# A two-layer graph network on one core: an early scatter into a small array, and a later one spread over five chunks

## What is computed

```python
# layer 0
h1..h4 = per-node-type linear maps of x              # 3125 x 64 each
w5e    = per-edge-type linear map of the 16 edge features
num    = sum(h3[dst] * (h4[src] + w5e), -1)
score  = softmax over an axis of length 1
out0   = h1 + segment_sum(score * (h2[src] + w5e), dst)
x      = layernorm(x + out0)
# layer 1
m      = relu(x[src] + edge_attr_32 @ We + be) + 1e-7
agg    = segment_sum(m * softmax_of_segment(m, dst), dst)
x      = layernorm(x + (x + agg) @ Wm + bm)
```

## Time and profile before

| | |
|---|---|
| runs | 2237.88, 2248.02, 2254.48 us; median 2248.02 |
| profiled execution | 2247.74 us, of it the span 2245.8 us |
| busy share of the span | TensorE 78%, VectorE 71%, GpSimd 58%, ScalarE 34% |
| mean granted TensorE clock | 0.886 |

### The profile page before, as it was taken

One profiled execution on the slowest core, in us unless ns is written; L12 is line 12 of the kernel. 1 busy time (PEld: TensorE's weight loads), 2 busy tenths in 40 slices (PEclk: granted clock), 3 DMA queues, 4 the chain that ended last, 5 costly groups with the idle time before them and its releaser, 6 DMA issues.

```text
span 2245.8 us, 29209 instructions
## 1 busy us (share of the span) xinstructions
PE 1747.1 (78%) x9112; PEld 1108.5 (49%) x9112; DVE 1602.6 (71%) x3058; ACT 757.1 (34%) x1397; POOL 1294.3 (58%) x1348
## 2 busy tenths in 40 slices
PE   6453889898889889888873487888878787878873
PEld 5222556665666556555662144454445444544442
DVE  7422677777777777677768377788778786878786
ACT  3100222222222222222222144455455545455461
POOL 6365555555666565565633666666666665656624
PEclk9876999999999999999986688899999998989885
DMA  8942444545554555454443145555545555545442
GB/s 274 369 96 83 131 137 134 156 134 154 138 150 141 144 145 144 137 146 133 139 133 93 39 117 148 148 161 153 148 147 150 150 148 143 152 144 151 144 151 57
DMA packets 220072, 323.65 MB, mean 144 GB/s; under 512 B 62802, under 2 KB 127948, under 8 KB 219789
## 3 DMA queue, kind: packets, MB, share of 16 engines
q1 hardware_dynamic: 132958, 150.94, 22.9%
q0 software_dynamic: 43056, 68.05, 13.7%
q10 hardware_dynamic: 43904, 102.79, 12.6%
HBM read 188.35 MB, written 133.22 MB: 143 GB/s over the span
## 4 chain that ended last, share of the span: by engine, by line
PE 28%; issue 17%; another core or an unknown queue 16%; ACT 12%; DVE 12%; ACTq 3%; POOL 2%; DMA 1%; DVEq 0%; SPq 0%; POOLq 0%
PE wide L957 8%; PE wide L1069 5%; ACT block L860 3%; PE wide L931 3%; PE wide L966 2%; ACTq L853 2%; ACT prob_wide L837 2%; PE wide L923 2%; ACT msg L838 2%; ACT block L841 1%; DVE h3d L1363 1%; PE bank L1005 1%; ACT block L830 1%; DVE featm L1354 1%
## 5 line engine op out<-in xcount | busy, mean ns | idle before, releaser
L672 POOL DMA_INDIRECT rows<-d_x,idx x588 | 559.7, 952 | 350.2 <-issue 155.3
L662 POOL DMA_INDIRECT block<-d_h,idx x482 | 462.9, 960 | 302.9 <-issue 126.8
L1069 PE MATMUL wide<-late,ntype_i 125*128 125x512 bf16 x975 | 240.4, 404 | 54.7 <-DVE ntype_i L1492 49.5
L662 POOL DMA_INDIRECT rows<-d_h,idx x160 | 153.8, 961 | 151.6 <-PE wide L931 58.3
L1363 DVE TENSOR_TENSOR_SCAN h3d<-keep,h3d,bank 128x512 f32<-128x512 bf16 x98 | 124.9, 1275 | 159.1 <-issue 114.4
L1069 PE MATMUL wide<-edge_lists,ntype_i 125*128 125x512 bf16 x936 | 229.2, 401 | 11.9 <-issue 11.5
L931 PE MATMUL wide<-typed,zeros 128*128 128x128 f32 (+1 forms) x1364 | 185.0, 283 | 13.1 <-issue 13.1
L1080 PE MATMUL wide<-ident,block 128*128 128x128 f32 x784 | 134.4, 320 | 72.0 <-ACT block L860 43.9
L1069 PEld LDWEIGHTS wide<-late,ntype_i 125*128 125x128 bf16 x975 | 101.1, 104 | 176.2 <-DVE ntype_i L1492 49.9
L957 PE MATMUL wide<-late,ntype_i 125*128 125x512 bf16 x702 | 177.1, 409 | 12.5 <-issue 5.0
L957 PE MATMUL wide<-edge_lists,ntype_i 125*128 125x512 bf16 (+1 forms) x702 | 170.7, 396 | 11.6 <-issue 9.2
(11 more groups left out here) (255 smaller groups left out, 3214.2 us busy)
## 6 DMA issues: line engine op xcount, KB each, us to landing
d_run<-block ACTq DMA_DIRECT2D x98, 512.0 KB
d_inj<-zeros SPq DMA_DIRECT2D x28, 896.0 KB
inj<-d_inj SPq DMA_DIRECT2D x98, 256.0 KB
d_run<-stage ACTq DMA_DIRECT2D x98, 256.0 KB
feat<-in_ea16x3T SPq DMA_DIRECT2D x196, 96.0 KB
types<-d_type SPq DMA_DIRECT2D x196, 64.0 KB
keep<-d_keep SPq DMA_DIRECT2D x196, 64.0 KB
keep<-d_pen SPq DMA_DIRECT2D x196, 64.0 KB
```

What stands on the lines that cost most here:

```text
L662: pool.indirect_dma_start(out=ring[c % RING][:, j, h, :], out_offset=None, in_=d_h24, in_offset=bass.IndirectOffsetOnAxis(ap=idx[:, c, at: ...
L672: pool.indirect_dma_start(out=rows1[c % RING1][:, j, h, :], out_offset=None, in_=d_x1, in_offset=bass.IndirectOffsetOnAxis(ap=idx[:, c, at ...
L1069: ins = pe.matmul(p_hot[s], table[q][:, SPLIT * k:SPLIT * (k + 1), :].rearrange("p b c -> p (b c)"), hot[s][:, k, :], start=(k == 0 and q ...
```

## The change

`d_early` is a second array with rows for the first 14 chunks alone (`EARLY`), cleared by 4 transfers ahead of the others (`EARLY_UNITS`). GpSimd scatters all 25 tiles into it (`early_i`; nodes whose first edge is elsewhere go to a dump row) ahead of every gather, and chunks 0 to 13 load their `inj` from it. `d_inj` loses the clearing of its first 4 transfers' rows, has 10 cleared in the head, and the last 14 in SyncE's loop, two behind each of chunks 2 to 8. The scatter into `d_inj` is 25 further DMAs, five behind the gathers of each of chunks 8 to 12. The rows of zeros are sent as 512 pieces of 448 values instead of 128 of 1792. `PICK_LEAD` falls from 4 to 2 and `FIRST_STEP` from 3 to 0. `load_pick(u)` stands ahead of the other loads of its chunk instead of behind them. ScalarE's copy of the weights into the tile of zeros waits for nothing of the clearing, and VectorE's three operations on `table` in the head stand later.

```diff
-AHEAD = 6
-ZEROS_EARLY = 7
+ZEROS_EARLY = 3
+ZEROS_LATE = 14
+EARLY = 14
+EARLY_UNITS = 4
+SCATTER_BEHIND = {c: (5 * n, 5 * n + 5) for n, c in enumerate(range(8, 13))}
...
-PICK_LEAD = 4
+PICK_LEAD = 2
...
-FIRST_STEP = 3
+FIRST_STEP = 0
...
+            no_rows = zeros[:, 0:7 * C].unsqueeze(1).to_broadcast([P, 4, 7 * C])
+
+            def clear(first, behind):
+                for z in range(first, behind):
+                    sp.dma_start(flat[z], no_rows).then_inc(s_injzero, 16)
...
-            for z in range(ZEROS_EARLY):
-                sp.dma_start(flat[z], zeros[:, :]).then_inc(s_injzero, 16)
+            for z in range(EARLY_UNITS):
+                sp.dma_start(flat_early[z], no_rows).then_inc(s_early, 16)
+            clear(EARLY_UNITS, EARLY_UNITS + ZEROS_EARLY)
...
+            def load_inj(s, r, c):
                 wait(sp, injT[s], r)
+                if c == EARLY:
+                    sp.wait_ge(s_inj, 2 * 16 * NT)
...
             for c in range(2, CHUNKS):
                 s, r = c % 2, c // 2
-                load_features0(s, r, halves(c))
-                load_inj(s, r, c * (2 * CH))
-                load_keep(s, r, halves(c))
                 for u in range(PICK_LEAD + 1, UNITS):
                     if c == max(2, UNTIL[u - LISTS] + 1):
                         load_pick(u)
+                load_features0(s, r, halves(c))
+                load_inj(s, r, c)
+                load_keep(s, r, halves(c))
+                clear(min(ZEROS_LATE + 2 * (c - 2), ZEROS), min(ZEROS_LATE + 2 * (c - 1), ZEROS))
...
+            pool.wait_ge(s_sel, KT)
+            pool.wait_ge(s_early, 16 * EARLY_UNITS)
+            pool.wait_ge(s_rows_i, 1)
+            scatter(d_early, early_i, 0, NT)
             pool.wait_ge(s_h24, 16 * 6)
-            for c in range(AHEAD):
+            for c in range(CHUNKS):
                 gather0(c)
...
+                if c in SCATTER_BEHIND:
+                    pool.wait_ge(s_injzero, 16 * (ZEROS - EARLY_UNITS))
+                    pool.wait_ge(s_inj, 16 * NT)
+                    scatter(d_inj, first_i, *SCATTER_BEHIND[c])
```

More of the change, by code:

```diff
@@ L177, in gnn_program @@
         first_i = sb("first_i", [P, NT], i32)
+        early_i = sb("early_i", [P, NT], i32)
         mid_i = sb("mid_i", [NP, 2], i32)
@@ L1270, in _ @@
             dve.wait_ge(s_mbcol, 1)
-            dve.wait_ge(s_rounded, 2)
-            dve.tensor_tensor(table[2][:, 0:NT, :], left0, table[1][:, 0:NT, :], ALU.subtract).then_inc(s_left, 1)
+            for q in range(3):
+                then(dve.memset(table[q][:, NT:, :], 0.0))
             dve.wait_ge(s_shift, 1)
```

61 lines of the change are left out of this document (26 added, 35 removed).

## The result

The changed kernel took 2436.76 us in the median (2433.59 to 2437.19, 3 runs), 1.0841 times the kernel before, 95% interval [1.0775, 1.0908]. The forecast was 2298 us, at most 2345: the sign was right, and 139 us were missing. The profiled execution has a span of 2431.8 us against 2245.8.

What follows compares the result with a forecast made beforehand. The prediction held the loop bound by TensorE, with VectorE close, and the head by a line of DMA issues. From 2247.7 us, -50 + 71 + 14 + 15 = +50 gave 2298 us, range 2240 to 2345.

Steps and rivals of the forecast that it cites:

- the start is thus 89 us earlier: Head: with the early scatter ahead of the gathers, TensorE can start chunk 1 at 116.5 instead of 205.6 us.
- can start chunk 1 at 116.5: Head: chunk 1's gathers issued at 115 us plus 1.7 us for landing let TensorE start then.
- not counted again: Head: the old pause of 15.6 us behind TensorE's first turn was left out of the changed kernel's start.
- The rival on it: Head: the 15.6 us pause comes back, tied to the loop's first matmuls; 2314 us, chance 0.12.
- GpSimd stands still for 30 us: Late scatter: GpSimd, done gathering chunk 8 at 175 us, waits for the last clearing until 205.
- the term of -50 at chunk 13: Head and late scatter together: chunk 13 at 278.6 instead of 328.5 us; bounds -65 and -25.
- The 25 extra scatters cost nothing beyond chunk 13: Loop: their 32 us are free, since GpSimd needs 8.1 us a step and TensorE over 10.
- List loads, +71: Layer 0 loop: list loads waiting for one-hots delay features, 28 steps from 4.3 to 6.8 us; bounds +38 and +127.
- the clock, +15: TensorE's clock falls after idle stretches, one in three of the 28 late-feature steps; between 0 and +48.
- More picks in the loop, +14: Picks move into steps 0 to 5 and 93; three steps of 5.8 us take 10.5; +9 to +15.
- Effects at nothing: ScalarE's copy of the weights, VectorE's shifted operations and the smaller pieces of zeros were priced without effect.
- the loop goes at TensorE's pace: Layer 0 loop: TensorE, busy 723 of 818 us, sets the step of 10.5 us, VectorE closely tied.

Runs made afterwards that it cites:

- e4: Kernel before without GpSimd's head waits on shift, column sum, row of H and picked units (gathers and scatter); ratio 1.0093.
- e11: Kernel before without GpSimd's head waits, with four fills (some 1.6 us) behind every eighth indirect DMA of the first 8 chunks and the scatter; ratio 0.9987.
- e3: Changed kernel with twelve fills behind every eighth GpSimd indirect DMA of layer 0's first 14 chunks and the scatters; 2389.95 us, ratio 1.0755.
- e7: Changed kernel with lists loaded behind features, rows of 28 chunks scattered first, second scatter in twos behind chunks 16 to 28; 2269.46 us, ratio 1.0123.
- e15: e9 with GpSimd held to 4 chunks ahead throughout and the second scatter behind chunks 11 to 35; 2223.3 us, ratio 0.9984.
- e9: e7 with 35 chunks first, single late scatters behind chunks 14 to 38, four-fill pauses to chunk 44, lead limited to 4, 5, then 8; 2237.67 us, ratio 1.0046.
- e10: e9 without the fills, so GpSimd pauses only where its lead is limited; 2252.02 us, ratio 1.0109.
- e13: e9 without the second scatter, rows of chunks from 35 on left out, so another output; ratio 0.9965.
- e18: Kernel before, head waits replaced by four-fill pauses, 4 chunks gathered ahead of the scatter, lead 4 until chunk 47, growing to 8 from chunk 72; ratio 1.0061.
- e1: Changed kernel with layer 0's pick lists loaded behind the chunk's features, rows and keep again; 2301.07 us, ratio 1.0365.
- e2: Kernel before with layer 0's pick lists loaded ahead of the chunk's features, rows and keep; 2317.29 us, ratio 1.0412.
- e12: Kernel before without GpSimd's head waits, with one fill (some 0.4 us) behind every eighth indirect DMA of the first 8 chunks and the scatter; ratio 1.0116.
- e5: e7 with four fills (some 1.6 us) behind every eighth indirect DMA of the first 14 chunks and the scatters; 2257.03 us, ratio 1.0079.

## Why the forecast missed

**Head, "the start is thus 89 us earlier": failed.** The times of GpSimd's list were nearly right (first scatter at 66.25 us where the list was forecast ready at 65, first gather at 104.4 where 97 was forecast). What failed is that TensorE "can start chunk 1 at 116.5": its `project0` of chunk 1 came at 192.0. The sum had followed data and taken GpSimd's waits on `picked[0]`, `s_shift`, `s_mbps` and `s_h3` for order alone, so that their removal cost nothing. One of them was GpSimd's only pause in 114 us. e4 (remove them: 15.6 us later), e11 (put pauses without meaning in their place: 28.7 us earlier than e4) and e3 (54 us earlier than the changed kernel) show it. The text had the right thread in hand, the 15.6 us for which "no row says what is waited for", and dropped it with "not counted again"; "then nothing runs until 202.9" was a misreading, for GpSimd issued its gathers until 197.9. The rival on it tied the pause to the first matmuls and priced it at 16 us.

**"GpSimd stands still for 30 us", then its pace: failed in size and kind.** It waited 67.2 us, from 203.9 to 271.15 us (forecast: 175 to 205): the clearing stands behind chunk 8's loads, and the chunks ran 75 us late. And what followed was not GpSimd's pace of 14 to 16 us a chunk but a stretch of 97 us without a pause and 84 us for one chunk. With both, the term of -50 at chunk 13 became +81.5. e7, which has no such stretch, has no such hole.

**"The 25 extra scatters cost nothing beyond chunk 13": wrong in the same way**, though hidden here by the hole. GpSimd's free time in the loop proved no slack: from chunk 13 to 30, 18 or 19 further indirect DMAs cost e15 and e7 some 1.2 us each though no stretch there was longer than 13 us, and where the lead grew (e9, e10, e13, e18) the extra ones cost 1.3 to 1.9 us each on the mean, with a standstill in it.

**List loads, +71: right in mechanism and near in size.** With the clock, +15, the forecast had 86 for what e1 measured as 108.6 in this kernel and e2 as 83.0 in the kernel before. The clock's part was at most 28, against 15. The steps of SyncE's list are as told: SyncE idle at the list load, the mask released by features.

**More picks in the loop, +14: not seen.** e1 has those picks and needs 818.2 us from chunk 13 to 92, where the kernel before needs 825.2 and its other variants without late scatters (e4, e12) 819.9 and 817.9. The last steps, where the term was to show, have 3 us of it at most: 92.7 us from chunk 86 to 97 before, 95.4 in e1. The forecast of +100 for this stretch (71 + 14 + 15) met the measured 926.8 - 825.2 = +101.6 partly by luck: the delay and the clock came out higher, and this term at nothing. (28 x 2.5 is 70 and not 71, which changes nothing.)

**Effects at nothing.** ScalarE's copy, VectorE's shifts and the smaller pieces of zeros are in every variant of the changed kernel and were not tried apart, so no run prices them.

**What stays open.** Why TensorE, VectorE and ScalarE stand still. A want of instructions is out (e4), and so are full DMA engines (busy at 0.11 to 0.20 in the standstills of e4 and of the changed kernel). The Trainium skill (SBUF — State Buffer, Who interferes with whom) has VectorE and GpSimd share a pair of ports, for which, with some of VectorE's instructions, the one that comes second waits, and says that TensorE and ScalarE never wait on anyone. Here GpSimd kept its rhythm of 1.25 us and the others stood, TensorE and ScalarE with them, so that rule doesn't explain these traces. Nor is it settled whether the loop's pace of 0.60 to 0.65 indirect DMAs a us (66 in 108 us before, 196 in 313 in e10, 98 in 151 in e9) is a limit of GpSimd's, of its wait for TensorE, or of standstills too short to be seen; a kernel with fewer gathers would tell, and none was run. In the forecast "the loop goes at TensorE's pace" is thereby in doubt.

## What to carry to other kernels

A wait in GpSimd's list may be worth something for its pause alone: before removing one, count how long GpSimd then issues indirect DMAs on end, and look at TensorE's "issue" idle time there. Price each indirect DMA that moves into a tuned loop at no less than its issue, even where GpSimd looks idle, and let GpSimd's lead over the consumer neither be longer than needed nor grow by several chunks on end. On a queue, a load that waits for a late event belongs behind every load that is due sooner.

## What the runs showed of the hardware

- Indirect DMAs issued by GpSimd back to back (one in 1.25 us) bring the other engines to a near standstill. In the loop TensorE's matmuls came singly from 12 to 22 us after the start of the stretch (e10: 444.6 to 456.9; e18: 795.4 to 809.3; e3: 344.7 to 363; after: 271 to 293), in the kernel before 21 us (134.4 to 155.3), in the heads of after and e4 38 and 54 us (66.3 to 104.5, 84.8 to 138.7). It was over 4 to 12 us behind the end of the stretch, and it can break off within one: at 163.4 us in the kernel before, and from 149.8 to 160 us in the head of e1, whose stretch ran from 66.4 to 170.6. The stretches of the loop before (230 to 1160 us) are some 10 us long at most, apart from one of 15, and there TensorE has no idle time above 2.1 us that is put down to "issue".
- Another stop is not of this kind: from about 101 to 125 us TensorE stands in the kernel before and in every kernel made from it, those with pauses too (e11: 101.5 to 125.7). The clearing transfers are issued ahead of it, and the DMA engines are busy at 0.91 to 0.98 in it (102 to 125 us in all these kernels), against 0.11 to 0.20 in the standstills; its cause wasn't tried.
- In the head of the kernel before, a pause of 0.4 us in ten did not help and one of 1.6 us did (e12, e11). In the changed kernel 1.6 us helped in part (chunks 2 to 4 of e5; e13), and with 4.7 us no such stop was left in the head (e3).
- A plain DMA of GpSimd of the same 128 rows takes 0.55 us (27.46 / 50) instead of 1.28, and TensorE works through 50 of them.
- In a standstill the granted clock falls as well: 0.52 in the hole, 0.63 in the head.
